# The order of two VectorE instructions in an attention block: row maxima of scores and the low halves of the probabilities

## What is computed

```
qkv    = layernorm(x) @ W_qkv + b_qkv
scores = (q @ k.T) / sqrt(32)
probs  = softmax(scores)              # per head, 1024 x 1024
ctx    = probs @ v
x      = x + ctx @ W_o + b_o
x      = x + (silu(h @ W_gate.T) * (h @ W_up.T)) @ W_down.T,   h = layernorm(x)
```

## Time and profile before

| | us |
|---|---|
| median of 3 runs (lowest to highest) | 2996.03 (2995.73 to 2997.73) |
| the profiled execution | 2997.6 |
| its span, first to last instruction | 2995.8 |
| TensorE busy | 2950.7 |
| VectorE busy | 2178.2 |
| ScalarE busy | 1659.7 |
| GpSimd busy | 1394.3 |

### The profile page before, as it was taken

One profiled execution on the slowest core, in us unless ns is written; L12 is line 12 of the kernel. 1 busy time (PEld: TensorE's weight loads), 2 busy tenths in 40 slices (PEclk: granted clock), 3 DMA queues, 4 the chain that ended last, 5 costly groups with the idle time before them and its releaser, 6 DMA issues.

```text
span 2995.8 us, 39212 instructions
## 1 busy us (share of the span) xinstructions
PE 2950.7 (98%) x13728; PEld 2336.6 (78%) x13728; DVE 2178.2 (73%) x3175; ACT 1659.7 (55%) x3039; POOL 1394.3 (47%) x998
## 2 busy tenths in 40 slices
PE   7999999999999999999999999999999999999999
PEld 6777777777777777777777878888788888888887
DVE  6788888888788888888885588866666656555653
ACT  2488778778888888888774143333333333332221
POOL 1346555554555555456562244444354443535730
PEclk9999999999999999999999999999999999999999
DMA  5545445454454554644846736522632223857874
GB/s 205 173 131 163 146 139 184 125 177 123 126 167 145 152 164 142 191 139 144 256 138 188 232 110 205 182 106 102 236 126 104 101 98 115 269 176 250 265 245 131
DMA packets 328376, 492.10 MB, mean 164 GB/s; under 512 B 34746, under 2 KB 178234, under 8 KB 320116
## 3 DMA queue, kind: packets, MB, share of 16 engines
q1 hardware_dynamic: 328180, 489.60, 51.4%
HBM read 318.58 MB, written 169.87 MB: 163 GB/s over the span
## 4 chain that ended last, share of the span: by engine, by line
PE 90%; DVE 6%; DMA 1%; ACT 1%; POOL 1%; issue 1%; SPq 1%; DVEq 0%; ACTq 0%; POOLq 0%
PE ps L901 20%; PE ps L902 20%; PE ps L903 20%; PE ps L985 7%; PE ps L969 7%; PE ps L997 7%; PE ps L1002 7%; DVE mx L1342 1%; DVE pl L1364 1%; DVE wl L1316 1%; PE ps L935 1%; SPq L1634 1%; DVE bl L1427 0%; DVE gl L1433 0%; DMA braw<-b_d 0%
## 5 line engine op out<-in xcount | busy, mean ns | idle before, releaser
L1551 POOL TENSOR_TENSOR pl<-pu,ph 128x512 fp32r<-128x512 f32 x504 | 679.7, 1350 | 674.0 <-ACT ph L1124 673.8
L1342 DVE TENSOR_REDUCE mx<-ps 128x1 f32<-128x512 f32 x1024 | 694.3, 684 | 164.6 <-PE ps L969 158.7
L1123 ACT ACTIVATE pu<-ps 128x512 f32<-128x512 f32 x1024 | 617.7, 603 | 278.3 <-PE ps L985 275.6
L1124 ACT ACTIVATE ph<-ps 128x512 fp32r<-128x512 f32 x1024 | 617.0, 603 | 0.0
L1364 DVE TENSOR_TENSOR pl<-pu,ph 128x512 fp32r<-128x512 f32 x520 | 425.3, 819 | 71.2 <-ACT ph L1124 69.5
L901 PE MATMUL ps<-bh,gh 128*128 128x512 f32 x1208 | 471.1, 390 | 5.6 <-DVE bl L1427 2.5
L903 PE MATMUL ps<-bl,gh 128*128 128x512 f32 x1208 | 470.1, 389 | 0.0
L902 PE MATMUL ps<-bh,gl 128*128 128x512 f32 x1208 | 470.0, 389 | 0.0
L969 PE MATMUL ps<-kst,qst 128*128 128x512 f32 x1024 | 404.1, 395 | 5.1 <-DMA qst<-qst 2.8
L985 PE MATMUL ps<-qst,kst 128*128 128x512 f32 x1024 | 404.4, 395 | 4.2 <-ACT ph L1124 4.2
L997 PE MATMUL ps<-ph,vt 128*65 128x512 f32 x1024 | 407.8, 398 | 0.7 <-ACT uu L1130 0.6
(11 more groups left out here) (143 smaller groups left out, 5166.3 us busy)
## 6 DMA issues: line engine op xcount, KB each, us to landing
graw<-in_wgu SPq DMA_DIRECT2D x42, 1024.0 KB, 5.2
sraw<-a_d SPq DMA_DIRECT2D x56, 704.0 KB, 4.9
qst<-q_d SPq DMA_DIRECT2D x192, 128.0 KB
kst<-k_d SPq DMA_DIRECT2D x192, 128.0 KB
a_d<-hs SPq DMA_DIRECT2D x88, 256.0 KB, 2.1
traw<-in_wd SPq DMA_DIRECT2D x77, 256.0 KB, 5.2
tt<-in_wd SPq DMA_DIRECT2D x77, 256.0 KB, 5.5
q_d<-stg SPq DMA_DIRECT2D x64, 256.0 KB, 2.5
```

Of the source, the lines that this page charges most:

```text
L1123: e.activation(pu[sl][:, :], bk[:, :], ACT.Exp, scale=SCALE).then_inc(s["a_p"], 1)
L1124: e.activation(ph[sl][:, :], bk[:, :], ACT.Exp, scale=SCALE).then_inc(s["a_ph"], 1)
L1342: e.reduce_max(mx[:, j % 2, t, half:half + 1], ps[bank_of["a", j, t, half]][:, :], AX.X).then_inc(s["v_mx"], 1)
L1551: e.tensor_tensor(pl[sl][:, :], pu[sl][:, :], ph[sl][:, :], ALU.subtract).then_inc(s["g_pl"], 1)
```

## The change

In each unit, `scores()` of tile u+24 goes ahead of the step "pl" of tile u-1 instead of behind it.

```diff
         step("p", j, t, half)
         rest.append((j, t, half))
+        n = u + 2 * AHEAD
+        if n < last:
+            scores(n // 16, n // 2 % TT, n % 2)
         if len(rest) > 1:
             pend.append(rest.pop(0))
             step("pl", *pend[-1])
-        n = u + 2 * AHEAD
-        if n < last:
-            scores(n // 16, n // 2 % TT, n % 2)
         due()
         if len(pend) > LAG:
             context(*pend.pop(0))
```

## The result

| | before | after |
|---|---|---|
| median of 8 runs, us | 2995.32 | 3004.47 |
| lowest to highest | 2994.35 to 2997.73 | 3001.21 to 3010.06 |
| profiled execution (span) | 2997.6 (2995.8) | 3002.66 (3000.8) |
| ratio, 95% interval | | 1.0029, 1.0020 to 1.0038 |

The change makes the kernel 0.29% slower, 8.7 us by the ratio. A later group on another occasion gave 1.0029 again (1.0018 to 1.0041). The runs of after lie 9 us apart, the first eight of before 3.4 us, but 33 later runs of before also lie 9 us apart (2991.55 to 3000.53 us), so the scatter need not be a mark of the new order.

What follows compares the result with a forecast made beforehand. TensorE, busy 98% of the span, was taken as the bound, with VectorE's `mx` costing it near 10.7 us. Terms -7.6 + 0.5 + 1.0 + 1.6 = -4.5 us took 2996.0 to 2991.5 us, range 2986.5 to 2997.5.

Steps and rivals of the forecast that it cites:

- Term 1: Attention stretch: `mx` ahead of `pl` removes TensorE's stalls for `mx`, eight longest looked up; -7.6 us, a ceiling.
- Term 2: Attention stretch: `pl` goes 0.6 us later, so L1002's weight loads may wait; +0.5 us, between 0 and 1.8.
- Term 3: Attention stretch: VectorE stands for its own unit's score before `mx` and `pl`; +1.0 us, between 0 and 9.6.
- Term 4: Attention stretch: vanished stalls uncover second scores' waits for ScalarE's `ph`; +1.6 us, between 0 and 7.6.
- The missing term: collisions: Rival: later `pl` starts inside GpSimd's next low part; about 10 us more stalls, +7 net, 3003 us; chance 0.05.
- the waits of VectorE for scores: Sign: VectorE's waits for L969 in the attention stretch rise well over 158.7 us.
- those of `pl` for `ph`: Sign: VectorE's waits for `ph` before `pl` fall from 69.5 us to little.
- the mean of `pl` as the mark of the rival: Sign: VectorE's mean `pl` falls from 819 ns if blocks are shortened, rises if the collision rival is right.
- L1002: Sign: L1002's waits for `pl` stay under 2 us.
- nothing beyond 1605 us: Sign: from 1605 us on nothing changes in the profile.
- TensorE's waits for `mx`: Sign: TensorE's waits for `mx` at L976, L969 and L901 fall from 7.3 us to 2 or 3.
- those of L985: Sign: waits of L985 for `ph` rise by 1 or 2 us.

Runs made afterwards that it cites:

- e3: Kernel before, but VectorE waits for this unit's score before it begins `pl`; 1.0024 of before, +7.2 us.
- the guard: GpSimd's low part waits until VectorE's `pl` of the tile before is done; 0.9975 of before in the new order, 0.9979 in the old.
- e13: Kernel before, with VectorE waiting for the unit's score before `pl` and GpSimd's low part waiting for VectorE's `pl` of the tile before; 1.0000 of before.
- e12: Kernel before, with GpSimd's low part waiting for VectorE's `pl` of the tile before; 0.9979 of before.
- e2: Kernel after, with GpSimd filling odd low tiles with zeros instead of subtracting; 0.9969 of before.
- e1: Kernel before, with GpSimd filling odd low tiles with zeros instead of subtracting; 0.9969 of before.
- e9: Kernel after, with GpSimd's low part waiting for VectorE's `pl` of the tile before; 0.9975 of before.
- e6: Kernel after, with each maximum taken over 256 of the 512 columns; 0.9956 of before.
- e5: Kernel before, with each maximum taken over 256 of the 512 columns; 0.9959 of before.
- the first pair: Kernels before and after, both with GpSimd filling odd low tiles with zeros instead of subtracting; both 0.9969 of before.
- e7: Kernel after, but the maximum goes ahead only where VectorE is backlogged, 94 of its 520 `pl`; 0.9981 of before, 5.7 us faster.

## Why the prediction was wrong

The forecast was 2991.5 us in a range of 2986.5 to 2997.5; 3004.47 came. The runs give three sizes, the first to some 3 us and the others, differences of two or more ratios, to 4 or 5 us, and only if they add, which was not tested beyond the pairs above:

- the hold, without the maximum ahead: +7.2 (e3), +6.3 with the guard (e13 less e12);
- the maximum ahead, with no collisions added: the order with the guard is -7.5 + 6.3 = -1.2 us, so the maximum ahead gives 1.2 + 6.3 = 7.5 us back;
- collisions: what is left of +8.7, that is 8.7 - 7.2 + 7.5 = 9 us; by the guard, which is worth 16.2 - 6.3 = 9.9 us more in the new order than in the old.

The pairs agree that the order by itself costs nothing once these blocks are gone or few: new less old is 0.0 us with the filling (e2 less e1), -1.2 with the guard (e9 less e12) and -0.9 with half maxima (e6 less e5).

**Term 1 (mx earlier, -7.6)** was right in mechanism, as six of the eight stalls went, and by this account in size, 7.5; at 4 us either way the close match may be luck.

**Term 2 (pl later at L1002, +0.5)** held: waits of L1002 for VectorE's `pl` are 1.1 against 0.7 us.

**Term 3 (VectorE held, +1.0 between 0 and 9.6)** was mis-sized: it measures 6 to 7 us. I took the lower end "because the great majority of pairs have that idle time". An average idle time of 0.55 us says nothing about the pairs that have none. That those few, where deferred work comes right behind the pair, set the price is likely, but the stalls of e3 were not followed one by one.

**Term 4 (ScalarE takes back 1.6)** did not come: L985 waits 4.0 us for `ph`, as before.

**The missing term: collisions.** This is the step that failed. They stood among the rivals with the right mechanism and nearly the right price, +10 us against the 9 to 10 measured, but with a chance of 0.05 and no place in the sum. Two sentences let them out. "Only just in reach" judged the shift by one pair: over all pairs the start moved from 1.38 to 0.32 us ahead of GpSimd's next low part, which is less than the 0.68 us that a `pl` lasts. "Where VectorE starts first it is GpSimd that waits" is what happened, 324 times, and the 73 us of it look harmless (weight loads of L1002 wait 0.3 us for GpSimd's `pl`, 0.2 in before); but in 88 other pairs GpSimd was the first. By number the rival was near: 71 new blocks with the next tile, while 40 of the old ones with the tile before went. Each now lasts longer, since it begins nearer the start of GpSimd's, as at 305.60. In time `pl` rose by 30 us in all, less than half of the 65 priced, and with the hold on top that was enough. The rival's own sum kept 3 us of term 1 and no hold; the cost came from both together.

Of the signs named, right were the waits of VectorE for scores, those of `pl` for `ph`, the mean of `pl` as the mark of the rival, L1002, and nothing beyond 1605 us. Wrong were TensorE's waits for `mx` and those of L985.

What stays open: the first pair and the guard show that low parts that meet are needed for the loss. Why the guard gains as much as 6.3 us in the old order, where it takes away 17 blocks of VectorE, was not tried apart. That the two block each other by an exclusive lock on a shared port pair is the word of the Trainium skill (SBUF — State Buffer, section "SBUF: two separate sides"). The traces agree, in both directions: 102 `pl` of VectorE that began inside GpSimd's took over 0.9 us in after, and 324 of GpSimd's began inside VectorE's, with a mean of 1578 ns against 1344 for the rest, while `mx`, which reads PSUM, stayed at 0.695 us at most, and the fillings of e1 and e2, which read nothing, neither waited for a `pl` nor held one up.

## What to carry to other kernels

When a step of one engine is moved, look at its phase against the other engine with which it collides, not only at its slack: a start that comes about 1 us later can put it into the other's operation, and both get longer. An order that puts a wait for fresh work first holds everything behind it; here it paid where the engine was already backlogged (e7), cost 8.7 us when made everywhere, and with the guard neither paid nor cost (e9 against e12). A semaphore wait on the engine with room (GpSimd, at half load) that keeps the two apart was worth more than either order.

## What the runs showed that was not expected

An added wait made the kernel faster: GpSimd stood 610.8 us for VectorE in e9 in place of 604.9 for ScalarE in after, did the same 504 subtractions in 80 us less, and the whole ran 16 us faster. And a reduction put one unit further from its matmul, with four PSUM banks in turn, cost 40 us with VectorE's busy time unchanged (2182.3 against 2178.2 us).
